# One recurrent attention and FFN layer: a new plan for the order of work inside an attention turn

## The reference

```
xn = layernorm(x)
# attention: 32 heads of 32 features, 8 key/value heads, rotary positions, causal mask
q, k, v = rope(xn @ wq.T), rope(xn @ wk.T), xn @ wv.T
s = softmax(q @ k.T / sqrt(32) + causal) @ v @ wo.T
# ffn: a small recurrence on the last token of each sequence
thought = layernorm(xn)[:, -1] @ agg_w + agg_b
for _ in range(4):
    t = gelu(layernorm(thought) @ d1_w + d1_b)      # 1024 -> 4096
    thought = thought + t @ d2_w + d2_b             # 4096 -> 1024
g = silu(layernorm(xn + sigmoid(xn @ gate_w + gate_b) * (thought @ bc_w + bc_b)))
out = x + s * g
```

## Time and profile before

| | us |
|---|---|
| median of 3 runs | 2773.43 |
| profiled execution, its own time | 2770.51 |
| its span, first to last instruction | 2768.4 |
| TensorE busy in the span | 2584.0 |
| VectorE busy | 1759.4 |
| GpSimd busy | 1369.4 |
| ScalarE busy | 1032.5 |
| mean granted clock of TensorE | 0.981 |

### The profile page before, as it was taken

One profiled execution on the slowest core, in us unless ns is written; L12 is line 12 of the kernel. 1 busy time (PEld: TensorE's weight loads), 2 busy tenths in 40 slices (PEclk: granted clock), 3 DMA queues, 4 the chain that ended last, 5 costly groups with the idle time before them and its releaser, 6 DMA issues. The chain is left out here.

```text
span 2768.4 us, 45646 instructions
## 1 busy us (share of the span) xinstructions
PE 2584.0 (93%) x14400; PEld 1717.1 (62%) x14400; DVE 1759.4 (64%) x3577; ACT 1032.5 (37%) x1650; POOL 1369.4 (49%) x627
## 2 busy tenths in 40 slices
PE   5999999979999999999999999999959999999998
PEld 4888888864444444444444444444438888888886
DVE  6444444446666666667666676666747777777777
ACT  2111111104555555555555555555531111111111
POOL 1111111125898878888788887889821111111111
PEclk9999999988999999999999999999979999999999
DMA  6444444445644645545456454464566555666556
GB/s 243 174 171 171 171 171 174 160 151 183 193 147 153 192 126 176 166 149 180 129 174 190 127 179 154 147 192 149 160 199 124 114 114 115 124 132 121 114 114 121
DMA packets 228288, 432.05 MB, mean 156 GB/s; under 512 B 16472, under 2 KB 98520, under 8 KB 228176
## 3 DMA queue, kind: packets, MB, share of 16 engines
q1 hardware_dynamic: 154784, 378.74, 41.6%
q0 software_dynamic: 73392, 51.91, 12.6%
HBM read 316.56 MB, written 113.51 MB: 155 GB/s over the span
## 5 line engine op out<-in xcount | busy, mean ns | idle before, releaser
L882 DVE CUSTOM_DVE_ANT_0 bcast<-mxp,mask_q 128x128 f32<-128x128 f32 (+7 forms) x1054 | 754.0, 754 | 422.7 <-PE mxp L998 274.2
L799 ACT ACTIVATE pr<-stp 128x512 f32<-128x512 f32 x1152 | 667.1, 598 | 557.6 <-PE stp L1007 313.5
L1007 PE MATMUL stp<-qs,ks 97*128 97x512 f32 x1152 | 504.0, 451 | 31.1 <-ACT pr L799 24.5
L426 PE MATMUL eo<-xt,w 128*128 128x512 f32 x1920 | 449.3, 393 | 3.6 <-DVE xt L369 3.6
L750 POOL TENSOR_TENSOR acc<-acc,pr 128x2048 f32<-128x2048 f32 x96 | 439.1, 4574 | 14.2 <-ACT pr L799 9.8
L426 PEld LDWEIGHTS eo<-xt,w 128*128 128x128 f32 x1920 | 359.2, 189 | 77.5 <-issue 4.0
L1007 PEld LDWEIGHTS stp<-qs,ks 97*128 97x128 f32 x1152 | 211.5, 188 | 315.1 <-ACT pr L799 157.7
L1370 PE MATMUL gp<-g,xa 128*128 128x512 f32 x1536 | 355.9, 391 | 17.1 <-DMA xa<-xt_scratch 17.1
L1370 PE MATMUL op<-o,ya 128*128 128x512 f32 x1536 | 355.6, 391 | 10.9 <-DVE ya L1313 10.9
L1370 PEld LDWEIGHTS gp<-g,xa 128*128 128x128 f32 x1536 | 290.0, 189 | 78.4 <-DMA xa<-xt_scratch 17.9
L1370 PEld LDWEIGHTS op<-o,ya 128*128 128x128 f32 x1536 | 289.8, 189 | 71.7 <-DVE ya L1313 11.3
(11 more groups left out here) (139 smaller groups left out, 2878.8 us busy)
## 6 DMA issues: line engine op xcount, KB each, us to landing
wch<-in_d_w SPq DMA_DIRECT2D x132, 1024.0 KB, 10.1
qs<-q_scratch SPq DMA_DIRECT2D x201, 256.0 KB, 7.3
xa<-xt_scratch POOLq DMA_DIRECT2D x66, 512.0 KB, 6.1
xt_scratch<-xt SPq DMA_DIRECT2D x16, 2048.0 KB, 14.4
q_scratch<-r SPq DMA_DIRECT2D x64, 512.0 KB, 3.2
yr<-y_scratch POOLq DMA_DIRECT2D x33, 512.0 KB, 5.8
xs<-in_x SPq DMA_DIRECT2D x33, 512.0 KB, 5.5
y_scratch<-ys SPq DMA_DIRECT2D x65, 256.0 KB, 2.0
```

The lines of the kernel that those rows point to most:

```text
L426: last = nc.tensor.matmul(out, lhs[a](k), rhs[c](k), start=(k == 0 and (a, c) == (0, 0)), stop=(k == KT - 1 and (a, c) == (1, 0)))
L799: nc.scalar.activation(pr[half][:, :, at:at + P], stp[u % 2][:].rearrange("p (h t) -> p h t", h=REP), ACT.Exp, scale=SCALE).then_inc(act_d ...
L882: last = nc.vector.tensor_tensor_reduce(out=bcast[:, k % 2, hh * step:hh * step + w], in0=mxp[k % 2][:, hh * step:hh * step + w], in1=mask ...
L1007: last = nc.tensor.matmul(bank, ks[par][:, j * P:(j + 1) * P], qs[par][:, :, i * P:(i + 1) * P], start=True, stop=i != j)
```

## The change

The plan's text is written anew; no function changes and no entry is added or dropped. Blocks that stood together in one slot are put in slots of their own, and the maxima move by up to two slots. In the plan before, slots 2, 6, 9, 13, 17, 21, 26 and 34 hold fp32 matmuls (eight stretches, the longest with four blocks); in the plan after, slots 1, 3, 6, 9, 11, 13, 16, 18, 21, 23, 26, 28, 31 and 34 do (fourteen). Behind the inversion `rc 0` stood two maxima in slot 22, and there is one now.

```diff
 0: mx 20
-1: cy 1
-2: pv 1 6, pv 1 7, fa 0, fa 1, fc
-3: mx 21
+1: pv 1 6, pv 1 7, cy 1
+2: mx 21
+3: fa 0, fa 1, fc
 5: mx 0
 6: mt 1, pv 0 0
 7: mx 1
 8: mx 2
-9: fb 0, fb 1, fs, pv 0 1
-11: mx 3
-12: mx 4, cy 0
-13: ft, pv 0 2, pv 0 3
+9: fb 0, fb 1, fs
+11: mx 3, pv 0 1, pv 0 2
+12: mx 4
+13: ft, pv 0 3, cy 0
 14: mx 5, ls
 15: mx 6
-16: mx 7
-17: ss 1, rc 1, pv 1 0
+16: ss 1, rc 1
+17: mx 7
+18: pv 1 0
 19: mx 8, l0, lc, ge
 20: mx 9
-21: ss 0, rc 0, pv 1 1
-22: mx 10, mx 11
-23: mx 12
-24: mx 13, l1, lv
-25: mx 14
-26: mt 0, pv 1 2
-27: mx 15
-28: mx 16
-29: mx 17
-31: mx 18
-32: lt
-34: pv 1 3, pv 1 4, pv 1 5
-35: mx 19
+21: ss 0, rc 0
+22: mx 10
+23: mx 11, pv 1 1, pv 1 2
+24: mx 12, l1, lv
+25: mx 13
+26: mt 0
+27: mx 14
+28: mx 15, pv 1 3
+29: mx 16
+30: mx 17
+31: pv 1 4
+32: mx 18, lt
+34: mx 19, pv 1 5
```

## The result

The changed kernel takes 2711.3 us (median of 4 runs, 2710.1 to 2712.9); the kernel before took 2773.8 beside it (2772.7 to 2776.0). The ratio is 0.977, with a 95% interval of 0.976 to 0.978, against a forecast of 2712 us.

A forecast was written before the change was run, and what follows sets the result against it. TensorE was taken to bound the kernel, with 5.7 us of waits in a 41.8 us turn. Sixteen pairs gaining 4.2 us give 67, less 6 at long turns, so 2773.4 - 61 = 2712 us, range 2682 to 2755.

The forecast's parts named there:

- The price of a stretch: On TensorE each fp32 stretch costs 0.30 us beyond its blocks; six more cost 1.8 us a turn, 58 us in 32.
- The waits fall from 5.7 us to 0.7: TensorE's waits in an ordinary turn shrink to two places, slot 6 (0.3 us) and slot 20 (0.4 us); turn 38.85 us.
- Rival C: Waits on VectorE's chain move instead of going, and six switches come on top: 2831 us, chance 0.10.
- D: Half the gain is lost at places with under 0.1 us of slack, about 1 us a turn: 2744 us, chance 0.13.
- The gelu comes onto the path for 1.7 us: ScalarE's table loads and gelu delay the score of slot 23 in every second turn: 1.7 us in 16 turns, 27 us.
- rival B: The gelu stays hidden because VectorE is late at that place anyway: 27 us less, 2685 us, chance 0.15.
- GpSimd's idle time covers the shorter turn: GpSimd waits 5.46 us before its first addition; the shorter turn takes 2 to 3 of these, at no cost.
- The long turns: At step ends maximum 21, now in slot 2, is ready about 1.6 us before VectorE: 1.6 x 4 = 6 us lost.
- The clock: Ordinary turns, with 5.7 us of pauses, never fell below clock 1.00 and will have fewer pauses, so it stays 1.00.
- Rival A: The clock falls once in each gelu turn, at slot 22: 1.7 us x 16 = 27 us, 2739 us, chance 0.12.

The follow-up runs named there:

- e5: Version e4 with two more fp32 stretches split (slot 11 over 11 and 12, slot 23 over 23 and 24), sixteen stretches: 2705.4 us, 0.975.
- e1: fp32 blocks as in the kernel after (13 stretches), maxima as in the kernel before: 2798.1 us, 1.008 against before.
- e2: Maxima as in the kernel after, fp32 blocks in the 8 long stretches of the kernel before: 2753.3 us, 0.992 against before.
- e3: The kernel after with a copy in place of the gelu, so without its two table loads: 2676.0 us, 0.964 against before.
- e9: The kernel before with a copy in place of the gelu, so without its two table loads: 2776.6 us beside 2778.2, 1.000.
- e4: The kernel after with the gelu's entry moved from slot 19 to slot 22: 2685.1 us, 0.968 against before.
- e10: The kernel before with two products moved from the three-block stretch of slot 34 into slot 31, nine stretches: 2773.0 us, 0.999.
- e6: Version e4 with two products of slot 11 moved into the stretch of slot 13, thirteen stretches: 2688.2 us, 0.969 against before.
- e8: Version e4 with one product moved from slot 31 into the stretch of slot 34, thirteen stretches: 2686.2 us, 0.968 against before.
- e7: Version e4 with maximum 7 made in slot 16 ahead of the inversion, not in slot 17 behind it: 2725.5 us, 0.982 against before.

## Why the prediction was right

In the ordinary turns the mechanism was right. At the ends of the steps a term was too small and in part another thing held the turns up. The two errors went in opposite directions, and the total came out right.

1. *The price of a stretch* (0.30 us): right. Behind a score it is 0.33 to enter, 0.99 for block and exit, 0.34 behind the next score, in after as in before, and e5 buys two for about 0.6. That entry behind a maximum costs no more was my choice between 0 and 0.2, and e5 bears it out.
2. *The waits fall from 5.7 us to 0.7*: right in kind and still too careful. The visible waits of an odd turn are 0.16 in slot 6 and 0.27 in slot 20, where I had 0.3 and 0.4. Odd turns take 38.46 to 38.51 us and not 38.85, even ones 40.25 to 40.30 and not 40.55, so a pair gains 4.83 and not 4.2. e1 and e2 show that the blocks or the maxima alone would not have done it. Rival C (the waits only move) falls, since the table of waits has none of them left, and so does D (half of the gain lost at tight places).
3. *The gelu comes onto the path for 1.7 us*: right. The wait is 1.58 in all 16 turns, 25.3 us in sum. With e3 it goes, e9 shows that it was hidden before, and rival B (it stays hidden) falls. With e4's placement it is largely hidden again.
4. *GpSimd's idle time covers the shorter turn*: right. Before its first large addition it waits 2.8 us in the even turns, forecast 2 to 3.5, and 4.3 in the odd ones, which is more than forecast.
```profile
1401.29 4.58 POOL L751 TENSOR_TENSOR acc<-pr 128x2048 f32<-128x2048 f32 x1 [2.79 <-ACT pr L800]
```
5. *The long turns*: the step that was mis-sized, and in good part for another reason than the one it gave. I had 1.6 us for maximum 21 at four steps, 6 in all. The jump is taken three times, and maximum 21 waits 1.31, 0.33 and 0.31 us, 2.0 in all. Yet each long pair gains 3.4 us less than an ordinary pair (272.1 to 267.8 us for the three, a gain of 4.3 where 3 x 4.83 = 14.5 were due), 10.2 in all. What the step left out are two stops behind the jump: TensorE's of up to 3.1 us, 8.3 in sum, and VectorE's of up to 4.3 us, which before had too and hid beside TensorE's long stretch; maximum 0 now waits 1.12 and 1.77 us behind it. Before, the long stretch of slot 34 covered TensorE's stop, and e10 shows that it did. The long pairs also have 6.8 us more at half clock, which cost 3.4. How the 10.2 divide is not shown, and the stop alone does not tell it: e4 has the same 8.3 us of stops, and its long pairs gain only 4.5 less than three of its ordinary pairs would. No row of before shows TensorE's stop. I looked at the step's end only for which result comes last, and not for what TensorE has queued across the jump when its last stretch gets shorter, nor for when VectorE gets going behind it.
6. *The clock*: the prediction leaned on the turn with 5.7 us of short pauses that kept 1.00, and read from it that such a turn never falls. The trace of before bears that out, but those of e9 (the same plan) and e10 (two blocks moved) do not. In e9 and in e10 the clock fell in two of 25 ordinary turns each, with no pause over 0.73 us in the turn, and each fall cost 1.6 us (43.3 and not 41.8). The 19 runs of before beside them point the same way: they go from 2768.4 us at a mean granted clock of 0.982 to 2787.7 at 0.974. This is one of the falls in e9:
```profile
845.90:849.30 3.40, 3.40 (x15) 0.74 (x13) 1.36 (x4) 1.18 (x2) 3.40 (x3) 0.50 0.00 0
```
So the rule of the Trainium skill that the prediction weighed ("TensorE: Matmul & The Clock Gate", section "A second HAM failure mode: psum-queue depth-cycling": many small pauses are enough) holds now and then for the old plan. It did not work against the change, as had been feared: the odd turns of after, with the most switches and the fewest pauses, kept 1.00 throughout, and so did every ordinary turn of e3, e4, e5, e6 and e8. Rival A, one fall in each turn with a gelu, came in part: the same stop of 1.58 us was followed by a fall in 2 of 16 such turns (676.1 and 1891.3), which then took 41.96 and 41.88 us, 1.7 more. With more stops of 0.8 to 1.4 us beside it the clock fell in 9 of the 25 ordinary turns of e1 and in 5 of the 13 even ones of e7. So the price of 1.7 was right and its frequency wrong.

The sum by measured terms: 16 pairs by 4.83 are 77 us; less 10.2 at the ends of steps and 3.4 for two falls of the clock leave 64. The 32 turns of the trace are 64.4 us shorter. The span is shorter by 60.4 only, because 0.6 us are lost ahead of the first turn and 3.3 behind the last, where 3.4 us more are spent at half clock. Against that stood 67 - 6 = 61: the waits gave 10 us more than forecast, and the step ends, the clock and the parts outside the turns took as much back. That the total came within 1 us of the forecast is luck; its terms were off by up to 10.

**What stays open.** That the stop for "issue" is the fetch of the code behind the jump is inferred. What is shown is where it stands, that it comes and goes with the length of the last stretch, and that the shorter jumps of the loop over chunks (over two turns of code, where the loop over steps has four) show none. The Trainium skill ("Runtime: NRT & Kernel Launch", section "Instruction fetch mechanics") says that a taken branch out of the loaded pages forces a fetch before work goes on; the 2.59 and 3.61 us on two engines agree with that, but no run took the jump away. And no run tells why the same stop, or the same short pauses, drop the clock in one turn and not in the next.

## What to carry to other kernels

When work is dealt out more finely, price the switch, and then ask of each other engine what it did under the long stretch that is now short. Here feeding VectorE evenly took 5 us of waits out of a turn for 1.8 us of switches, while ScalarE's table switch lost its cover, and so did the jump at the end of the loop. The table switch got its cover back by moving one entry to the longest stretch that is left (e4 brought 26 us by two lines). For the jump that did not pay (e8), since VectorE, late behind the jump on its own account, came next. And walk the first and last turn of a loop on their own: a model of the ordinary turn was within 1% here, and at the loop's ends it had 6 us for 10.

## What the runs showed of the hardware

- How long a tiny VectorE operation takes can hang on what GpSimd does beside it. In the kernel before, the instruction of line 851 on 128x32 values took 0.19 us at the shortest and 1.81 at the longest, and that of line 861 0.19 and 3.50, beside GpSimd's additions of up to 4.6 us. The Trainium skill ("SBUF — State Buffer", section "SBUF: two separate sides") calls this an exclusive lock on a pair of ports, for which an operation with two operands in memory waits out GpSimd's whole instruction. The rows agree: in after the operation of 3.27 us ends at 1296.13, and GpSimd's addition, 4.56 us from 1291.52, at 1296.08. That chain (1.93 + 3.49 us before, and 3.27 + 3.49 after) is one reason why the maxima behind the jump are late.
- Behind the jump of the outer loop TensorE stops for 2.1 to 3.1 us, unless the work queued ahead of it is long: with three fp32 blocks last, as before, no such stop is seen. VectorE stops for 3.6 to 4.0 us in before and for 3.6 and 4.3 at two of the three jumps of after. The jumps of the inner loop show neither.
- Each 3.4 us at half clock cost 1.5 to 1.7. In after they came behind stops of 1.1 us and more, and an equal stop does not always bring them, 2 times in 16 for 1.58 us. In the old plan they also came, 2 times in the 25 ordinary turns of e9 and as often in e10, where no pause was over 0.73 us.
